# Gated delta-rule recurrence: three score groups placed among the merges, and the queries' rotary tables made on chip

## The reference, cut to what matters

```python
angles = pos[:, None, None, None] * omega_scale[None, :, :, None] * inv_freq
cos, sin = transpose(cos(angles)), transpose(sin(angles))        # per mode, position, head
qr = _l2norm(_rotary(q, cos, sin)) * scale
kr = _l2norm(_rotary(k, cos, sin))
def step(S, inp):
    q_t, k_t, v_t, b_g, b_beta = inp
    S = S * jnp.exp(b_g)[..., None, None]
    kv = jnp.einsum('mbhk,mbhkv->mbhv', k_t, S)
    dv = (v_t[None] - kv) * b_beta[..., None]
    S = S + k_t[..., :, None] * dv[..., None, :]
    return S, jnp.einsum('mbhk,mbhkv->mbhv', q_t, S)
mode_w = jax.nn.softmax(mode_logits, axis=-1)
o = jnp.einsum('tmbhv,hm->bthv', ys, mode_w)                      # the modes are weighed and added
```

## Time and profile before

| | |
|---|---|
| median of 3 runs | 4420.95 us (4414.33 to 4445.32) |
| the profiled execution | 4432.15 us, span of the core 4430.4 us |
| `project` | 0 to 276 us |
| `tables` | 276 to 391 us |
| start of `recurrence` to the first `run_TM` | 391 to 492 us |
| 63 steps from the first `run_TM` to the last | 492 to 3906 us |
| rest of the last step, and `experts` | 3906 to 4430 us |
| mean granted TensorE clock | 0.913 |

### The profile page before, as it was taken

One profiled execution on the slowest core, in us unless ns is written; L12 is line 12 of the kernel. 1 busy time (PEld: TensorE's weight loads), 2 busy tenths in 40 slices (PEclk: granted clock), 3 DMA queues, 4 the chain that ended last, 5 costly groups with the idle time before them and its releaser, 6 DMA issues. The chain is left out here.

```text
span 4430.4 us, 193545 instructions
## 1 busy us (share of the span) xinstructions
PE 3831.2 (86%) x85713; PEld 3139.3 (71%) x85713; DVE 3551.3 (80%) x6911; ACT 2886.0 (65%) x9736; POOL 378.6 (9%) x220
## 2 busy tenths in 40 slices
PE   5511799899989998999999999998999899979999
PEld 2201687778777877877787788787877788866666
DVE  5663898889888888989888989898888889835665
ACT  5752577667767776767677767676766677744443
POOL 1230000000000010100000000010000010000000
PEclk8755899999999999999999989999999999989999
DMA  4667222322232223222322232232223222121110
GB/s 115 168 172 174 60 62 56 93 58 57 56 94 56 57 65 86 69 57 66 86 56 56 71 80 57 56 83 68 56 56 80 70 56 64 49 66 32 34 34 8
DMA packets 319910, 314.39 MB, mean 71 GB/s; under 512 B 139865, under 2 KB 252385, under 8 KB 314977
## 3 DMA queue, kind: packets, MB, share of 16 engines
q1 hardware_dynamic: 319072, 302.00, 26.4%
HBM read 232.70 MB, written 69.21 MB: 68 GB/s over the span
## 5 line engine op out<-in xcount | busy, mean ns | idle before, releaser
L911 DVE TENSOR_TENSOR run_EL<-run_XL 128x30 f32<-128x30 f32 (+14 forms) x1920 | 644.0, 335 | 66.0
L912 DVE TENSOR_TENSOR run_XL<-run_XL,run_EL 128x30 f32<-128x30 f32 (+14 forms) x1920 | 637.7, 332 | 65.9
L1046 PE MATMUL run_SP<-run_KP 64*32 64x128 f32 x8192 | 630.7, 304 | 38.1 <-DVE run_KP L898 20.8
L979 POOL TENSOR_TENSOR run_DB<-run_DB,run_below 128x1024 f32<-128x1024 f32 x128 | 305.6, 2388 | 3257.4 <-DVE run_KP L898 1751.6
L1046 PEld LDWEIGHTS run_SP<-run_KP 64*32 64x32 f32 x8192 | 474.0, 120 | 119.4 <-issue 83.7
L798 ACT ACTIVATE run_DB<-run_DB,run_col 128x64 f32<-128x64 f32 x2048 | 541.5, 351 | 4.7 <-POOL run_DB L979 1.0
L874 DVE TENSOR_TENSOR run_SC<-run_SP,run_DB 128x512 f32<-128x512 f32 x512 | 340.7, 685 | 198.5 <-PE run_SP L1050 190.0
L805 ACT ACTIVATE run_KD<-run_PR,run_col 128x64 f32<-128x64 f32 x2048 | 480.6, 329 | 18.2 <-PE run_PR L1065 10.1
L1050 PE MATMUL run_SP<-run_KP 64*32 64x64 f32 x8192 | 471.5, 244 | 1.2 <-issue 1.1
L811 ACT ACTIVATE run_R<-run_KS,run_col 128x64 f32<-128x64 f32 x1792 | 415.0, 324 | 64.4 <-PE run_KS L1073 64.1
L1008 PE MATMUL run_PR<-ident,run_win 128*64 128x128 f32 x4096 | 286.9, 283 | 174.4 <-DMA run_win<-KQ_s 152.4
(11 more groups left out here) (201 smaller groups left out, 7545.2 us busy)
## 6 DMA issues: line engine op xcount, KB each, us to landing
run_DB<-G_s SPq DMA_DIRECT2D x512, 128.0 KB, 3.0
run_EG<-EG_s SPq DMA_DIRECT2D x128, 512.0 KB, 6.8
run_tab<-TAB_s SPq DMA_DIRECT2D x128, 256.0 KB, 4.0
KQ_s<-proj_win SPq DMA_DIRECT2D x32, 768.0 KB, 7.4
run_win<-KQ_s SPq DMA_DIRECT2D x64, 384.0 KB, 3.3
TAB_s<-tab_tab SPq DMA_DIRECT2D x128, 128.0 KB, 2.4
run_V<-V_s SPq DMA_DIRECT2D x128, 128.0 KB, 3.2
V_s<-proj_vv SPq DMA_DIRECT2D x64, 128.0 KB, 3.1
```

Of the source, the lines that this page charges most:

```text
L911: v.link(dve.tensor_tensor(e, bcast(XL[:, r + 1:, r], 2, done), bcast(XL[:, r, 0:done], 1, rows), ALU.mult))
L912: less = dve.tensor_tensor(XL[:, r + 1:, 0:done], XL[:, r + 1:, 0:done], e, ALU.subtract)
L1046: pe.matmul(out[64 * e:64 * e + C, p].rearrange("p (z u) i -> p z (u i)", z=2), KP[f, key, p, t0:t1], KP[f, kq, p, t0:t0 + SPAN], start=Tr ...
```

## The change

Two things are changed.

1. On PE, score groups 3, 4 and 5 of sequence k + 1 now stand between the merges of sequence k: after `merge(k, 0, 0)`, after `merge(k, 0, 1)` and after `merge(k, 1, 0)`. Groups 4 and 5 leave the first two places. ACT's order at the head changes with it: ZM of half 0, `first_block(0)`, ZM of half 1, `first_block(1)`, XN of half 0.
2. `TAB_s` holds two planes a head instead of four. `tables` no longer makes or writes the weighed ones. The weights stay on chip (`weight`), and ACT makes the queries' planes in `recurrence` by eight instructions a head, `weigh(h, i)`, at its places of chunks 5 to 7 in the step before the head's first rotation (for head 0 in step -2, all eight at once). The first of them waits until the keys' planes have landed. SP loads four transfers, waits for them, and loads four more; it no longer waits for `rot_q`, but for the last `weigh` of the running head.

```diff
-        PE_PLACES = [["score 4"], ["merge", "score 5"], ["score 6"], ["score 7"], ["keys 0"], ["next 0"], ["keys 1"], [],
+        PE_PLACES = [[], ["merge"], ["score 6"], ["score 7"], ["keys 0"], ["next 0"], ["keys 1"], [],
...
-                      ["turn 0"], ["keys 4", "next 0"], ["keys 5", "turn 1"], ["keys 6", "next 1"],
-                      ["keys 7", "next 2"], ["turn 2", "next 3"], [], ["turn 3"]]
+                      ["turn 0"], ["keys 4", "next 0"], ["weigh 0", "keys 5", "turn 1"], ["weigh 1", "keys 6", "next 1"],
+                      ["weigh 2", "keys 7", "next 2"], ["weigh 3", "turn 2", "next 3"], ["weigh 4", "weigh 5"],
+                      ["weigh 6", "weigh 7", "turn 3"]]
```

```diff
                 for k in STEPS:
                     if real(k):
                         merge(k, 0, 0)
+                    prepare_part(k, "score 3")
+                    if real(k):
                         merge(k, 0, 1)
+                    prepare_part(k, "score 4")
                     if real(k):
                         merge(k, 1, 0)
-                    prepare_part(k, "score 3")
+                    prepare_part(k, "score 5")
```

```diff
+                def weigh(h, i):
+
+                    z, p = i // PAIRS, i % PAIRS
+                    if i == 0:
+                        act.wait_ge(l_tab, 128 * (h + 1))
+                        if h:
+                            act.wait_ge(rot_q, 2 * B * h)
+                    act.activation(tab[:, 2 + z, p], tab[:, z, p], ACT.Copy, scale=weight[:, h, p:p + 1]).then_inc(weighed, 1)
...
                         merged(k, 0, 0)
-                        merged(k, 0, 1)
                         act.wait_ge(xt_done, 2 * k + 2)
                         first_block(0)
+                        merged(k, 0, 1)
                         first_block(1)
                         merged(k, 1, 0)
```

```diff
-                def load_tab(h, ks):
-                    for k in ks:
+                def load_tab(h):
+                    for k in range(2):
                         for e in range(2):
                             for half in range(2):
                                 at = 64 * e + HALF * half
                                 sp.dma_start(tab[at:at + HALF, k], TAB_s[h, k, e]).then_inc(l_tab, 16)
-                            if h:
-
-                                sp.wait_ge(l_tab, 256 * h + 64 * k + 32 * (e + 1))
+                        if h:
+
+                            sp.wait_ge(l_tab, 128 * h + 64 * (k + 1))
...
                         sp.wait_ge(rot_k, 2 * (b + 1))
-                        sp.wait_ge(l_tab, 256 * (b // B + 1))
-                        load_tab(b // B + 1, (0, 1))
-                        sp.wait_ge(rot_q, 2 * (b + 1))
-                        load_tab(b // B + 1, (2, 3))
+                        sp.wait_ge(weighed, 8 * (b // B + 1))
+                        load_tab(b // B + 1)
```

More of the change, by code:

```diff
@@ L168, in _ @@
                 for e in range(2):
+                    rows = slice(64 * e, 64 * e + 64)
+                    v(dve.tensor_copy(weight[rows, :, :], modes[rows, :, e::2]))
+                for e in range(2):
                     for q in range(2):
@@ L509, in project, with tables @@
         fresh()
-def tables(nc, sems, fresh, c_pos, c_col, om_part, w_part, raw, COL_s, TAB_s):
+def tables(nc, sems, fresh, c_pos, c_col, om_part, raw, COL_s, TAB_s):
     with ExitStack() as ctx:
@@ L543, in _ @@
                     u = h % 2
-                    sp.wait_ge(done, 3 * (h + 1))
+                    sp.wait_ge(done, h + 1)
+                    sp.wait_ge(swung, 2 * h + 2)
                     for e in range(2):
@@ L555, in _ @@
                 for u in range(2):
-                    sp.wait_ge(put[u], 16 * 16 * (H // 2))
+                    sp.wait_ge(put[u], 16 * 8 * (H // 2))
                 sp.wait_ge(put_c, 16)
@@ L565, in _ @@
                     if h >= 2:
-                        dve.wait_ge(done, 3 * (h - 1))
+                        dve.wait_ge(done, h - 1)
+                        dve.wait_ge(swung, 2 * (h - 1))
                     for j in range(2):
@@ L582, in _ @@
                     if h >= 2:
-                        act.wait_ge(put[u], 16 * 16 * (h // 2))
+                        act.wait_ge(put[u], 16 * 8 * (h // 2))
                     act.activation(tab[:, u, 1], ang[:, u], ACT.Sin).then_inc(done, 1)
@@ L587, in _ @@
                     act.activation(tab[:, u, 0], turns[:, u], ACT.Sin, scale=-1.0, bias=col[:, 0:1]).then_inc(swung, 1)
[L588 to L594, removed]
-                    last.then_inc(done, 1)
                     if h < 3:
@@ L603, in tables, with recurrence @@
         fresh()
-def recurrence(nc, sems, fresh, c_mat, ident, KQ_s, V_s, G_s, EG_s, COL_s, TAB_s, O_s):
+def recurrence(nc, sems, fresh, c_mat, ident, weight, KQ_s, V_s, G_s, EG_s, COL_s, TAB_s, O_s):
     GROUP = SUPER // 2
@@ L725, in _ @@
                 load_win(0)
-                load_tab(0, range(4))
+                load_tab(0)
                 load_g(0, 0, l_ga)
@@ L823, in prepare_part @@
                     i = int(i)
+                    if kind == "weigh" and real(k + 2) and real(k + 3) and (k + 3) % B == 0:
+                        weigh((k + 3) // B, i)
                     if kind == "merge" and real(k):
@@ L835, in _ @@
                 for k in STEPS:
+                    if k == -2:
+                        for i in range(2 * PAIRS):
+                            weigh(0, i)
                     if real(k):
                         merged(k, 0, 0)
-                        merged(k, 0, 1)
                         act.wait_ge(xt_done, 2 * k + 2)
                         first_block(0)
+                        merged(k, 0, 1)
                         first_block(1)
@@ L950, in _ @@
                     if rotates:
+                        if b % B == 0:
+                            dve.wait_ge(weighed, 8 * (b // B + 1))
                         products(b, True, 0)
```

25 lines of the change are left out of this document (12 added, 13 removed).

## The result

The changed kernel takes **4370.35 us** (median of 3 runs, 4351.55 to 4386.89) against 4420.95: a ratio of 0.9891, interval 0.9852 to 0.993. It is faster by 1.1%, 51 us, where 181 were forecast, and lies above the range. The profiled execution took 4386.89 us; it is the slowest of the three.

The account below looks back on a forecast made before the run. It took PE's and DVE's loops, nearly equal, as the bound, PE's lengthened by clock falls. -112 (score order), -25 (heads), -7 (start), -37 (`tables`) make -181: 4432 to 4251, median 11 below, 4240 us; range 4160 to 4340.

Parts of the forecast that it names:

- part 1: Score groups among the merges on PE: a step without change of head goes from 53.3 to 51.3 us, -112 over 56.
- I take it that three falls in four go: PE's clock at the step's head: of 3.25 us lost a step, a quarter (0.8) stays; called a choice, not a reading.
- 51.3 less 0.8 of clock: Forecast step without change of head, 51.3 us, of which 0.8 is the clock loss expected to stay.
- 0.2 us of looser coupling: Term of the 51.3 us step: 0.2 us for what the looser coupling leaves.
- Rival B: PE's clock falls as before; the steps give 17 us instead of 112: 4335, range 4295 to 4360; chance 0.22.
- The 0.3 us for `take` 4: DVE at the step's head would wait 0.3 us for ACT's exponentials for chunk 4, where it waited 1.47 for scores.
- the relay: Step's head: PE waits for DVE's `take`, then XN, then `take` 4 for ACT; as a slower rival, 4514, chance 0.04.
- Part 2: A head's tables in `recurrence`: half the transfers and DVE's wait go, ACT weighs; -25 us over seven heads, ends 0 and -50.
- 6.5 us of new stall against 11.5 of the old one: At a change of head: ACT stands 5 us for the landing plus 1.5 for eight instructions, replacing DVE's 11.5 us wait.
- The start: Before the first step, half of DVE's wait for sixteen table transfers goes: -7 us (-3 to -10).
- Part 3: Stage `tables` ends at 353 instead of 390 us, with 11.5 MB to move instead of 19.9: -37 us (-30 to -40).
- The test named in the prediction: Signs: mean clock over the steps 0.97 or more, DVE's `run_SP` waits under 60 us, `run_DB` waits some 20.

Follow-up runs that it names:

- e4_exp4_early: Changed kernel with ACT making chunk 4's exponentials ahead of XN of half 0; time unchanged within the interval, wait for exponentials 29.4 us instead of 156.3.
- e13_first_wide: Changed kernel with only the first kind of merge matmul read over 64 rows, the second keeping 32; 4393 us, 379 us at half clock.
- e2_tables_only: Kernel before with the tables change alone, old order of score groups and ACT kept; it gave the whole gain, with 369 us at half clock.
- e9_wide_exact: Tables-only kernel with both kinds of merge matmuls over 64 rows, added rows zero so the output is exact; 4279 us.
- e10_mixed: Changed kernel with the second merge mixed by quarters with score group 3 and the third with group 4; 90 us more than the changed kernel.

## Why the prediction was wrong

**The step that failed** is in part 1: "I take it that three falls in four go." The clock's loss in a loop away from a change of head went from 2.94 to 2.27 us, by 0.67 instead of 2.4. Of 55 steps with a fall near their head 29 were left, and the stretches that remained were longer. The loops without half clock came as forecast in kind, 51.12 us in the mean of 19 against 51.3 less 0.8 of clock, 50.5; there are just too few of them. The view behind the choice was one step's head with PE busy 4.13 of 4.13 us; the falls were not followed over all 63 steps, where heads with idle time in them and stretches of 10 us or more would have shown that more than the length of pure merges is at work. A second term was missing: PE's own work and idle time, put at no change and 0.2 us of looser coupling, rose by 0.41 and 0.38 us a loop and took back what the clock gave.

**Rival B came nearest**: its 4335 (4295 to 4360) is too low by 35, since it still took 17 us from the order and 25 from the change of head, and both gave nothing. Its condition, that the clock falls as before, held only in part: a fifth of the time at half clock went (393 to 311 us). So the steps stood still by a balance that no rival had. The Trainium skill's page "TensorE: Matmul & The Clock Gate", section "HAM oscillation — how this bites in real kernels", ties such falls to TensorE's idle gaps. The traces agree in part. In the changed kernel the 13 steps with the longest gaps all have a fall. But before, 34 of the 39 steps that idle under 0.1 us have one too, and in the wide version with a gap in each of 62 steps, 48 have none. What a gap does here depends on the tiles around it.

**The 0.3 us for `take` 4** was 2.79, since PE arrives 5.8 us after `run_TM` and the third merge lasts longer. That e4_exp4_early took 127 us off this wait and none off the time shows that it cost nothing: the relay was the wrong thing to count.

**Part 2, -25, was 0.** The step that failed is "6.5 us of new stall against 11.5 of the old one". Of DVE's 80 us of waiting for tables 23 reached PE, as waits for `run_TM` at the end of the seven steps in which DVE waits (37.7 us in 8 waits in all, 14.6 of them ahead of the first step): 3.3 us each, not 11.5. These waits are gone. In their place PE waits 51.9 instead of 33.5 us for the keys by token, and idles more on its own, and so the 21 loops around a change of head took 55.98 us before and 55.96 after. ACT's standing was 13.2 us in five steps, not 35 in seven, and the eight multiplications cost nothing that can be told. **The start**, -7, was -9. **Part 3**, -37, was -40. Of the two ends that the forecast saw meet, the transfers' at 350 and DVE's at 351, the second decided. In the changed kernel DVE works on the angles from 277.9 to 339.8 us and waits 0.9 us in between for ACT; ACT waits 17.7 us for DVE and 10.1 for transfers; and the DMA queues are busy 0.65 of the stage. That halving the bytes was enough to get there is shown, that the bytes set the new end is not.

The test named in the prediction spoke clearly. The mean clock was 0.95 against the 0.97 that it asked for; DVE's waits for scores were 90.2 against "under 60", and those for `run_DB` 156.3 against 20. Of the two ways to be wrong that it named, PE's loop at the full clock is longer than 50.5 (51.1), and part of the falls did move to the fourth merge. Of the 31 steps with a fall in the first 14 us, 22 have it around the third merge (4 shortly ahead of it, 18 in it or behind), 4.6 to 7.7 us after the first, and 9 in the fourth or up to 1.5 us behind it, at 11.3 to 13.2; before, none began between 10 and 15 us.

What stays open: the rule by which neighbours and gaps decide a fall, why e13_first_wide has a lower clock than the changed kernel, and why the order alone lost 0.9% on the kernel before. The last goes with 9.6 us at half clock a loop around a change of head against 7.6, in one profile each.

## What to carry to other kernels

When one engine's loop sets the step, count that engine's work and stalls, and treat every wait of the others as slack until an experiment says otherwise: 294 us of waits, aimed at and removed, came back as 304. When a clock fall is to be argued away, tabulate it over all steps with what surrounds it first; then look at the rows that the matmuls use, since widening 32-row tiles to 64 with zeros took 84 us where reordering them took none. The stage `tables`, on the other hand, could be forecast within 3 us by following both the transfers and the engine that feeds them to their ends: taking bytes away helped only as far as that engine's work.

## What the runs showed that was not expected

- Doubling the rows that the 256 merge matmuls of a step read, with zeros, cut the time at half clock from 369 to 102 us at the same count of matmuls (e2_tables_only, e9_wide_exact).
- A change of shape between merges and scores costs PE about 0.1 us (e10_mixed).
- PE stalls for "issue" in the middle of merges. Counted in matmuls, those at the heads of steps 9 to 15 of the changed kernel stand 1397, 1271, 1270, 1271, 1398 and 1271 apart, where a step has 1300. So such a gap wanders through the head from step to step. It fits that like steps fall and don't fall; that it is the reason isn't shown.
